# Two-layer mixture of experts on one core: the end of layer two with three bf16 terms for the rows that TensorE spreads, rows in partition order, and gated biases made ahead

## What is computed

```python
def _L1_ffn_ref(x, Wg, W1, b1, W2, b2):
    xt = x.reshape(n, h)                      # n = 1024, h = 128
    S = jax.nn.sigmoid(xt @ Wg).T
    G, I = jax.lax.top_k(S, k)                # k = 256 rows of each of 8 experts
    ex = xt[I]
    hid = jax.nn.gelu(jnp.einsum('ekh,ehf->ekf', ex, W1) + b1[:, None, :], approximate=False)
    out = (jnp.einsum('ekf,efh->ekh', hid, W2) + b2[:, None, :]) * G[..., None]
    new_x = jnp.zeros_like(xt).at[I.reshape(-1)].add(out.reshape(-1, h))
    return new_x.reshape(b, l, h)
```

## Time and profile before

| | us |
|---|---|
| median of 3 runs | 155.68 |
| lowest and highest | 155.34, 156.07 |
| span of the profiled execution | 153.7 |
| median less that span | 1.98 |
| PE busy in the span | 141.9 (92%) |
| DVE busy | 92.6 (60%) |
| ACT busy | 82.2 (53%) |
| POOL busy | 57.3 (37%) |

### The profile page before, as it was taken

One profiled execution on the slowest core, in us unless ns is written; L12 is line 12 of the kernel. 1 busy time (PEld: TensorE's weight loads), 2 busy tenths in 40 slices (PEclk: granted clock), 3 DMA queues, 4 the chain that ended last, 5 costly groups with the idle time before them and its releaser, 6 DMA issues.

```text
span 153.7 us, 3561 instructions
## 1 busy us (share of the span) xinstructions
PE 141.9 (92%) x1100; PEld 123.3 (80%) x1100; DVE 92.6 (60%) x306; ACT 82.2 (53%) x247; POOL 57.3 (37%) x62
## 2 busy tenths in 40 slices
PE   7999698899999999999799997979997999999990
PEld 3847687799999999964689975748986888889990
DVE  0278957756655555450599777765531685754872
ACT  0596807667777765620367769985126344445000
POOL 0000277344477554461500000002677777773000
PEclk9999999999999999999999999999999999999998
DMA  5994517999999972112702940040122221656634
GB/s 155 346 407 164 138 42 227 383 345 343 402 389 341 294 254 96 34 55 84 209 0 110 394 184 0 4 145 2 28 44 59 56 55 52 188 179 183 191 87 136
DMA packets 19252, 26.15 MB, mean 170 GB/s; under 512 B 1970, under 2 KB 13618, under 8 KB 18850
## 3 DMA queue, kind: packets, MB, share of 16 engines
q1 hardware_dynamic: 16386, 21.73, 41.6%
q0 software_dynamic: 1760, 3.67, 8.0%
q10 hardware_dynamic: 1088, 0.52, 1.2%
HBM read 19.98 MB, written 5.93 MB: 169 GB/s over the span
## 4 chain that ended last, share of the span: by engine, by line
PE 68%; DVE 15%; issue 5%; DMA 4%; POOL 4%; DVEq 1%; ACT 1%; POOLq 0%
PE bank L573 12%; PE bank L583 12%; PE bank L741 11%; PE bank L652 10%; PE bank L751 5%; POOL xg L445 3%; PE bank L475 3%; PE bank L619 3%; PE bank L628 2%; DMA xg<-rows,idx 2%; DVE y L1050 2%; DMA picked<-y,sidx 1%; DMA got<-picked 1%; DVE hid L1145 1%; PE bank L498 1%
## 5 line engine op out<-in xcount | busy, mean ns | idle before, releaser
L849 ACT ACTIVATE hT<-bank,w_now 128x128 f32<-128x128 f32 x92 | 26.3, 368 | 12.9 <-PE bank L573 12.9
L573 PE MATMUL bank<-xg,w_now 128*128 (+1 forms) x184 | 24.7, 277 | 1.3 <-ACT xg L842 0.8
L423 POOL DMA_INDIRECT xs<-rows,gidx x15 | 14.6, 976 | 28.6 <-DVE gidx L1057 17.9
L926 ACT ACTIVATE h1T<-bank,c_sb 128x256 f32<-128x256 f32 x44 | 18.2, 473 | 12.5 <-PE bank L652 12.5
L583 PE MATMUL bank<-w_sb,hT 128*128 (+1 forms) x184 | 24.4, 276 | 0.3 <-ACT hT L849 0.3
L573 PEld LDWEIGHTS bank<-xg,w_now 128*128 128x128 f32 x184 | 22.4, 192 | 2.4 <-issue 1.8
L583 PEld LDWEIGHTS bank<-w_sb,hT 128*128 128x128 f32 x184 | 22.4, 192 | 0.5 <-ACT hT L849 0.5
L741 PE MATMUL bank<-v_sb,h1T 128*128 128x128 f32 x176 | 22.7, 280 | 0.0
L741 PEld LDWEIGHTS bank<-v_sb,h1T 128*128 128x128 f32 x176 | 20.9, 192 | 1.4 <-ACT h1T L926 1.2
L428 POOL DMA_INDIRECT picked<-y,sidx x16 | 15.6, 977 | 10.3 <-DVE y L1106 9.1
L445 POOL DMA_INDIRECT xg<-rows,idx x14 | 14.0, 1000 | 5.7 <-issue 3.4
(11 more groups left out here) (201 smaller groups left out, 231.5 us busy)
## 6 DMA issues: line engine op xcount, KB each, us to landing
v_sb<-in_v SPq DMA_DIRECT2D x16, 256.0 KB
cw_sb<-in_cond_w SPq DMA_DIRECT2D x8, 386.5 KB, 5.4
plane<-y SPq DMA_DIRECT2D x5, 512.0 KB, 5.5
w_sb<-plane SPq DMA_DIRECT2D x5, 512.0 KB, 5.1
w_sb<-in_w SPq DMA_DIRECT2D x2, 1024.0 KB, 8.3
w_sb<-in_w SPq DMA_DIRECT2D x1, 1290.0 KB, 7.0
w_sb<-in_w SPq DMA_DIRECT2D x1, 774.0 KB, 4.9
rows<-row SPq DMA_DIRECT2D x1, 544.0 KB, 3.4
```

Of the source, the lines that this page charges most:

```text
L423: pool.indirect_dma_start(out=xs[:, b % RING], out_offset=None, in_=rows0, in_offset=rows_at(gidx, b)).then_inc(gathered[b % RING], 16)
L573: mm = pe.matmul(bank[2 + j % 2][:, P * f:P * f + P], w1_now[:, j % WB_RING, P * f:P * f + P], xsT[:, bass.ds((j - e) * P, P)], start=True ...
L849: ins = act.activation(hT[:, j % 2, P * f:P * f + P], bank[2 + j % 2][:, P * f:P * f + P], ACT.Relu, bias=w1_now[:, j % WB_RING, F + f:F + ...
L926: act.activation(h1T[:, n % 2, fc], bank[UP_BANKS[(2 * n + h) % 4]][:, CAP * f:CAP * f + CAP], ACT.Gelu, bias=c1_sb[:, e * NF + fc:e * NF ...
```

## The change

The end of layer two is changed in five ways.

1. **Three bf16 terms.** A spread half of `y1` is split into three bf16 tiles (`thirds`) that sum to it: ACT rounds it to bf16 (first term), DVE subtracts that (`left`), ACT rounds the rest (second term), DVE subtracts again (third term). The one-hot matrices are bf16, made from an int16 ramp. PE runs three bf16 matmuls for each chunk of a half in place of one float32 matmul, all with the same one-hot block as weights: 96 in place of 32.
2. **Partition order.** `rows1` and the planes hold token (c, p) at row 8 p + c. What a partition reads or writes is then one piece of 4096 bytes (4352 in `rows1`). The index constants follow (`prow` = 8 p, `cval` = c).
3. **Gated bias ahead.** For each half, DVE makes bias times score in `gb`, one expert ahead (two for the first). `score` is then one instruction, PSUM times score plus `gb`, and PE waits for `y1_kept` in place of `y1_ready`.
4. **Planes.** Parts 0 and 1 are both added behind expert 4, and parts 2, 3 and 4 after all experts.
5. **Order of the terms.** DVE makes the terms of expert 5's halves ahead of the scores of expert 6, and those of expert 6 ahead of part 2.

```diff
@@ SP
-            load(rows1.rearrange("(c p) d -> p c d", p=P), row[:], rows1_written)
+            load(rows1.rearrange("(p c) d -> p c d", p=P), row[:], rows1_written)
-                load(part[e].rearrange("p (c d) -> p c d", d=C), plane[e].rearrange("(c p) d -> p c d", p=P), part_in[e])
+                load(part[e], plane[e].rearrange("(p c) d -> p (c d)", p=P), part_in[e])
@@ PE, down_e and spread_out
-                    pe.wait_ge(y1_ready, NH * (n - HEAD) + h - 2)
+                    pe.wait_ge(y1_kept, NH * (n - HEAD) + h - 2)
...
                     pe.wait_ge(spread_ready, n + 1)
-                    pe.wait_ge(y1_kept, NH * e + h + 1)
+                    pe.wait_ge(last_third, n + 1)
                     for c in range(NC):
-                        mm = pe.matmul(bank[SUM_BANKS[c // 4]][:, P * (c % 4):P * (c % 4) + P], spread1h[n][:, P * c:P * c + P],
-                                       y1[:, e % Y1_RING, h], start=(n == 0 and c % 4 == 0), stop=(n == SPREADS - 1 and c % 4 == 3))
+                        for k in range(3):
+                            mm = pe.matmul(bank[SUM_BANKS[c // 4]][:, P * (c % 4):P * (c % 4) + P],
+                                           spread1h[n][:, P * c:P * c + P], thirds[:, n, k],
+                                           start=(n == 0 and c % 4 == 0 and k == 0),
+                                           stop=(n == SPREADS - 1 and c % 4 == 3 and k == 2))
@@ ACT, behind the last gelu
+            for n in range(0, SPREADS, NH):
+                for m in range(n, n + NH):
+                    act.wait_ge(y1_kept, SCATTERS + m + 1)
+                    act.activation(thirds[:, m, 0], y1_of(m), ACT.Copy).then_inc(first_third, 1)
+                for m in range(n, n + NH):
+                    act.wait_ge(first_left, m + 1)
+                    act.activation(thirds[:, m, 1], left[:, m], ACT.Copy).then_inc(second_third, 1)
@@ DVE
+            def gated_bias(e):
+                v.wait_ge(gathered1[e], 16 * NH)
+                if e >= 2:
+                    v.wait_ge(y1_kept, NH * (e - 1))
+                for h in range(NH):
+                    v.tensor_scalar(gb[:, e % 2, h], c2b_sb[:, e], xg[:, e * NH + h, C + e:C + e + 1], None,
+                                    ALU.mult).then_inc(gb_ready, 1)
...
-                with_bias(HEAD + e, h)
-                v.tensor_scalar(y1[:, e % Y1_RING, h], yb[:, (HEAD + e) % 2, h], xg[:, e * NH + h, C + e:C + e + 1], None,
-                                ALU.mult).then_inc(y1_kept, 1)
+                v.wait_ge(gb_ready, NH * e + h + 1)
+                v.wait_ge(y1_sent, NH * (HEAD + e) + h + 1)
+                v.scalar_tensor_tensor(y1[:, e % Y1_RING, h], bank[y_bank(HEAD + e, h)][:, C * h:C * h + C],
+                                       xg[:, e * NH + h, C + e:C + e + 1], gb[:, e % 2, h], ALU.mult,
+                                       ALU.add).then_inc(y1_kept, 1)
+
+            def thirds_of(e):
+                for n in range(NH * e - SCATTERS, NH * e - SCATTERS + NH):
+                    v.wait_ge(first_third, n + 1)
+                    v.tensor_tensor(left[:, n], y1[:, e % Y1_RING, n % NH], thirds[:, n, 0], ALU.subtract).then_inc(first_left, 1)
+                for n in range(NH * e - SCATTERS, NH * e - SCATTERS + NH):
+                    v.wait_ge(second_third, n + 1)
+                    v.tensor_tensor(thirds[:, n, 2], left[:, n], thirds[:, n, 1], ALU.subtract).then_inc(last_third, 1)
...
+            gated_bias(0)
             for e in range(SPARSE):
+                if e + 1 < SPARSE:
+                    gated_bias(e + 1)
                 for h in range(NH):
                     score(e, h)
+                if NH * e >= SCATTERS:
+                    thirds_of(e)
...
-                if e in TAKEN_AT:
-                    take_part(TAKEN_AT[e])
-            for e in range(len(TAKEN_AT), PLANES):
+                if e == 4:
+                    take_part(0)
+                    take_part(1)
+            for e in range(2, PLANES):
                 take_part(e)
```

More of the change, by code:

```diff
@@ L63 @@
 _WIDTHS = [("ident", P), ("tri", P), ("iota", P), ("rev", E), ("pcol", 1), ("lt", NC * E), ("le", E),
-           ("slotj", NPAIR), ("dval", K * NC), ("cval", NC), ("same", P), ("coarse", 2), ("steps", STEPS), ("below", STEPS)]
+           ("slotj", NPAIR), ("dval", K * NC), ("cval", NC), ("prow", 1), ("same", P), ("coarse", 2), ("steps", STEPS), ("below", STEPS)]
 _AT, _n = {}, 0
@@ L103, in constants @@
     put("dval", (P * c + T * k).reshape(1, -1))
-    put("cval", P * np.arange(NC)[None, :])
+    put("cval", np.arange(NC)[None, :])
+    put("prow", NC * p[:, None])
     put("same", p[:, None] // NJ == p[None, :] // NJ)
@@ L223, in adaln_moe @@
         wd = sb("wd", [P, NC, DENSE])
-        iota_t = y0[:, NC:2 * NC].rearrange("p c d -> p (c d)")
-        spread1h = [w2_sb[:, 3 * T:4 * T], y0[:, 2 * NC:3 * NC].rearrange("p c d -> p (c d)"), hT[:].rearrange("p r f -> p (r f)"), w2_sb[:, T:2 * T]]
+        iota_t = y0[:, NC:NC + NC // 2].rearrange("p c d -> p (c d)").bitcast(I16)
+        spread_lo = y0[:, 2 * NC:3 * NC].rearrange("p c d -> p (c d)").bitcast(BF16)
+        spread_hi = hT[:].rearrange("p r f -> p (r f)").bitcast(BF16)
+        spread1h = [spread_lo[:, 0:T], spread_lo[:, T:2 * T], spread_hi[:, 0:T], spread_hi[:, T:2 * T]]
+        thirds = w2_sb[:, 3 * T:3 * T + SPREADS * 3 * C // 2].bitcast(BF16).rearrange("p (n k d) -> p n k d", n=SPREADS, k=3)
+        left = w2_sb[:, T:T + SPREADS * C].rearrange("p (n d) -> p n d", n=SPREADS)
         idx1f = sb("idx1f", [P, SPREADS])
@@ L272, in adaln_moe @@
         h1T = sb("h1T", [P, 2, NF, CAP])
-        yb = sb("yb", [P, 2, NH, C])
+        gb = sb("gb", [P, 2, NH, C])
         Y1_RING = NC // NH
@@ L319, in adaln_moe @@
         added = [sem(f"added_{e}") for e in range(E)]
-        xg_turned, xgT_ready, h1_ready, h1T_ready, y1_ready, y1_kept, y1_sent = (sem(n) for n in (
-            "xg_turned", "xgT_ready", "h1_ready", "h1T_ready", "y1_ready", "y1_kept", "y1_sent"))
+        xg_turned, xgT_ready, h1_ready, h1T_ready, gb_ready, y1_kept, y1_sent = (sem(n) for n in (
+            "xg_turned", "xgT_ready", "h1_ready", "h1T_ready", "gb_ready", "y1_kept", "y1_sent"))
+        first_third, first_left, second_third, last_third = (sem(n) for n in (
+            "first_third", "first_left", "second_third", "last_third"))
         zero_ready, zeroed, out_ready, out_done = sem("zero_ready"), sem("zeroed"), sem("out_ready"), sem("out_done")
@@ L336, in adaln_moe @@
         unit = [(True, SPARSE + d // CHUNKS, d % CHUNKS) for d in range(HEAD)] + [(False, e, 0) for e in range(SPARSE)]
-        TAKEN_AT = {4: 0, 5: 1, 6: 2}
         UP_BANKS = (2, 4, 5, 3)
@@ L437, in _ @@
             pool.memset(zero, 0.0).then_inc(zero_ready, 1)
-            pool.iota(iota_t, [[1, T]], base=0, channel_multiplier=0,
+            pool.iota(iota_t, [[1, NC], [NC, P]], base=0, channel_multiplier=0,
                       allow_small_or_imprecise_dtypes=True).then_inc(iota_ready, 1)
@@ L956, in _ @@
             act.activation(hlfv[:, :, :, 0].rearrange("p c e h -> p (c e) h"), hlf1h[:], ACT.Identity,
-                           scale=const("pcol")).then_inc(hlfv_ready[0], 1)
+                           scale=const("prow")).then_inc(hlfv_ready[0], 1)
             take_yd(1)
@@ L972, in _, with y1_of @@
                 gelu(n, 1)
+            def y1_of(n):
+                e, h = (SCATTERS + n) // NH, (SCATTERS + n) % NH
+                return y1[:, e % Y1_RING, h]
+            for n in range(0, SPREADS, NH):
[5 more added lines that the diff above has]
+                    act.activation(thirds[:, m, 1], left[:, m], ACT.Copy).then_inc(second_third, 1)
         @block.vector
@@ L1248, in spread_rows @@
                     v.tensor_scalar(spread1h[n], iota_t, idx1f[:, n:n + 1], None, ALU.is_equal).then_inc(spread_ready, 1)
-            def with_bias(n, h):
-                v.wait_ge(y1_sent, NH * n + h + 1)
-                v.tensor_tensor(yb[:, n % 2, h], bank[y_bank(n, h)][:, C * h:C * h + C], c2b_sb[:, unit[n][1]],
-                                ALU.add).then_inc(y1_ready, 1)
-                v.wait_ge(y1_ready, NH * (n - HEAD) + h + 1)
+            def gated_bias(e):
[5 more added lines that the diff above has]
+                                    ALU.mult).then_inc(gb_ready, 1)
             def score(e, h):
```

1 line of the change is left out of this document (removed).

## The result

| | before | changed |
|---|---|---|
| median of 5 runs, us | 156.0 | 154.75 |
| lowest and highest | 155.34, 156.09 | 154.64, 155.26 |
| span of the profiled execution | 153.7 | 152.8 |

The ratio of the changed kernel to the one before is 0.9943, with a 95% interval from 0.9921 to 0.9966: 0.6% faster (the two medians alone would give 0.8%). The ratio rests on five executions of each kernel. The forecast was 155.0 with a range from 154.2 to 156.3.

What follows compares the result with a forecast made beforehand. PE was taken to bound the end; its spread gives back 1.8 us, but DVE then bounds: last addition -0.73, outputs give back 0.05, so -0.7, span 153.0, time 155.0, range 154.2 to 156.3.

Steps and rivals of the forecast that it cites:

- PE's spread at 0.056 a matmul, 5.4 us: Spread at the end of layer two: 96 bf16 matmuls with hidden weight loads, ending at 148.4 where it was 150.17.
- rivals 2 and 3: PE's spread with weight loads partly in the open, time 156.3, chance 0.06; or altogether in the open, 159.3, chance 0.05.
- The bound moves from PE to DVE: At the end, PE alone gives back 1.8 us, but DVE then bounds and about 0.7 is left.
- The sum: Last DVE addition -0.73, 0.05 given back for closer output DMAs: -0.7 in all, span 153.0, time 155.0.
- Terms of expert 5 in time for PE: Before the spread: half 0 has its terms by 143.0, when PE is free, so PE does not wait.
- DVE's stretch: DVE's end: expert 6's terms by 145.15, three parts to 148.85, two additions to 150.15, against 150.88 before.
- the hops: Expert 6's four ACT copies and DVE subtractions after the last score: 0.36, 0.33, 0.36, 0.33, plus 0.1 for sharing engines.
- Part 1 at no cost: Addition ahead of expert 5: the load takes 3 to 4.3 us, landing at 137.6 to 139; cost nothing, with 0.0 to 0.2.
- the rival: Part 1 still late, landing at 140.55: PE spreads about 0.9 late, DVE ends at 151.0, time 155.7 to 155.9; chance 0.13.
- Parts 3 and 4: Loads for DVE's last additions, wanted at 146.3 and 147.6; part 4 lands about 147 or earlier; as late as before costs 0.2.
- The gathers: Gathers that release PE, their rows now 4352 bytes apart between partitions: taken as 0, with 0.2 either way.
- within 0.5%: Whole time the same as before, chance 0.55; faster, under 154.9, 0.36; slower, over 156.46, 0.09.

Runs made afterwards that it cites:

- with float32: Changed kernel with the float32 spread and one-hots of before and no bf16 terms: 155.95 us, ratio 1.0026 to the kernel before.
- with two terms: Changed kernel with two bf16 terms in place of three, the third neither made nor multiplied: 154.17 us, ratio 0.9916 to the kernel before.
- chunk-order kernel: Changed kernel with rows1 and the planes in chunk order as before, loads in pieces of 512 bytes: 156.4 us, ratio 1.0027 to the kernel before.
- the kernel with part 2 on POOL: Changed kernel with part 2 added on POOL after its last scatter: ratio 0.999 to the kernel before, on the disturbed chip.

## Why the prediction was right

- **PE's spread at 0.056 a matmul, 5.4 us.** Right to the thousandth (0.0558), and the loads hide: PE ended its spread at 148.2, and rivals 2 and 3 fall. The Trainium skill, page "TensorE: Matmul & The Clock Gate", section "Back-to-back issue gap", gives 81 ns for each matmul of 128 columns in a sustained stream of loads and matmuls. This stream ran at 55.8 ns, so here that figure does not hold.
- **The bound moves from PE to DVE.** Right, and shown from both sides: with float32 DVE waits 1.56 for PE; with two terms 1.8 us less of PE bring 0.74, nearly all of it DVE's own saving. One reading under it was wrong: that DVE was only 0.2 us behind PE. It was held by parts 3 and 4, and with them in time it has about 1.5 us. And one reason given was wrong: two parts behind expert 6 before and three now. Three stood there before too (144.16, 146.27 and 147.95). What is new in DVE's last stretch are the terms, and that the three parts follow each other without waiting. The sum did not use that count, so it is not touched.
- **Terms of expert 5 in time for PE.** Right: PE started at 142.66 with no idle time ahead.
- **DVE's stretch.** Predicted from A: the second sum at 10.7; measured 10.44. The term that was too large is the hops: a copy on ACT was 0.31 with 0.02 to 0.03 to each side, where I had 0.32 with 0.04, and the four hops after the last score took 1.33 us, not 1.45. The scores ended at A + 4.12, where I had 4.26.
- **Part 1 at no cost.** Right in the profiled execution, where its load took 3.8 us after 133.7 (predicted: 3 to 4.3 after at most 134.65). What I did not see is that its moment of issue hangs on the landing of expert 1's scatter, 3.3 us here, 4.2 in the kernel before and up to 5.8 in others. In the chunk-order kernel this made up 2.3 of the 3.0 us of delay. The chunk-order kernel shows that the price if late was sized well (A + 11.1; the rival had 151.0 for the second sum, A + 11.6, measured 11.7).
- **Parts 3 and 4.** They landed ahead of need, no idle time stands ahead of them.
- **The sum.** Here one step was wrong in kind, though small: I took the end of the span from the second sum and gave back 0.05 for the two output DMAs being closer. In fact the second sum came 1.0 earlier by A, the span ended only 0.7 earlier, since, as the table suggests, the first output's data now set the end. The two errors, -0.27 and +0.24, cancelled, so the -0.7 was met by luck in part. The span itself fell by 0.9, and 0.2 of that is only the earlier A.
- **The gathers.** Landing took 2.6 us in the median with rows in partition order and 2.5 in chunk order, which is inside what I allowed. The wait that they cause lies ahead of A, and its effect is too small to be told from the scatter of A.
- **The chances.** Most of the chance lay on "within 0.5%"; the measured 0.57% is just beyond, and the interval covers both.

## What to carry to other kernels

Where two engines end close to each other, cost every edit on both, and ask what the second one waits for: its own work or a late load. Taking 1.8 us from PE alone made the end 1.24 us longer. Three edits that together brought nothing without the bf16 terms were each worth the whole gain or more with them. Measure such effects from a point shortly ahead of them, not from the start: here spans scattered by more than the effect, and the distance from A repeated to 0.01 us in the changed kernel on two chips. Such a distance says what the edit does to the end, and only whole times say what it is worth. And when work is moved ahead of a chain because a load will be there by then, the worst landing of the load, and of the scatter that it waits for, belongs in the sum, not the usual one.

## What the runs showed of the hardware

- Rounding a tile on ACT and giving it back to DVE costs 0.31 us and 0.02 to 0.03 for each hand-over; a chain of four such hops on 128 x 128 takes 1.3 us.
- Loads of a 512 KB table in pieces of 4096 bytes landed after 3.3 to 4.3 us in the changed kernel, in pieces of 512 bytes after 4.1 to 7.0 in the kernel before. Over all profiles it was 3.1 to 5.3 us against 4.0 to 7.0. The slowest scatter beside them took 3.8 to 5.8 us with partition order and 5.6 to 6.4 with chunk order, on the undisturbed chips.
- A POOL addition of 1024 float32 columns took 2.46 and 2.37 us. While it ran in the kernel with part 2 on POOL, one DVE subtraction of two SBUF tiles of 128 x 128 took 0.86 us where its three like took 0.28 to 0.29, and ended 0.15 us after POOL's addition; the scores and the bias made beside it kept their length. That POOL is the cause was not tested.
- One-hots of 1024 columns from an int16 ramp to bf16 took 0.48 us on DVE, from float32 to float32 0.73 to 0.85.
